# A six-layer cross-attention kernel: sums turned in 32x32 blocks, and two batches at a time from the fourth layer on

## What is computed

```python
q = (norm(x) @ Wq + bq); k = ctx @ Wk + bk; v = ctx @ Wv + bv      # 16 heads of 16
p = softmax(q @ k.T * 0.25)                                        # per head
x = x + (p @ v) @ Wo + bo                                          # CROSS and L3: norm before, none behind
x = x + relu(norm(x) @ f_w1 + f_b1) @ f_w2 + f_b2                  # FFN
```

## Time and profile before

| what | us |
|---|---|
| median of three runs | 1397.02 |
| the profiled execution | 1397.33 |
| its span in the trace | 1395.6 |
| TensorE busy | 1329.5 |
| VectorE busy | 994.2 |
| ScalarE busy | 898.1 |
| GpSimd busy | 603.0 |

### The profile page before, as it was taken

How to read it: one execution, slowest core, us unless ns; L and a number is a source line. 1 busy time by engine, 2 the same in 40 slices (tenths; PEclk the granted TensorE clock), 3 DMA queues, 4 the chain that set the end, 5 groups by cost and what they waited for, 6 DMA issues and landing times.

```text
span 1395.6 us, 46148 instructions
## 1 busy us (share of the span) xinstructions
PE 1329.5 (95%) x20076; PEld 1138.8 (82%) x20076; DVE 994.2 (71%) x1842; ACT 898.1 (64%) x1519; POOL 603.0 (43%) x767
## 2 busy tenths in 40 slices
PE   5999999999999999999999999999999999899997
PEld 4777888777887878888788878888999999778885
DVE  4778777888788777767776788886664446767774
ACT  4777777777777756666566776776434435667764
POOL 4944544576644643443334342222686665111100
PEclk9999999999999999999999999999999999999999
DMA  7211100010100000000000110000000000001000
GB/s 283 76 31 35 31 13 10 24 31 25 38 9 9 10 25 3 3 2 2 3 2 25 33 31 16 9 9 24 9 9 1 2 1 15 10 32 39 17 25 32
DMA packets 16609, 35.11 MB, mean 25 GB/s; under 512 B 2071, under 2 KB 7447, under 8 KB 15895
## 3 DMA queue, kind: packets, MB, share of 16 engines
q1 hardware_dynamic: 16407, 32.16, 7.1%
HBM read 27.96 MB, written 4.19 MB: 23 GB/s over the span
## 4 chain that ended last, share of the span: by engine, by line
PE 67%; DVE 14%; ACT 8%; POOL 5%; issue 3%; DMA 2%; SPq 0%; DVEq 0%; POOLq 0%; ACTq 0%
DVE s_nm L1101 9%; PE ps L717 8%; PE ps L782 8%; PE ps L744 6%; PE ps L796 6%; PE ps L810 6%; PE ps L606 5%; PE ps L659 5%; PE ps L761 5%; PE ps L631 4%; ACT s_PU L952 4%; PE ps L618 4%; PE ps L595 2%; PE ps L722 2%; DVE s_KH L1058 2%
## 5 line engine op out<-in xcount | busy, mean ns | idle before, releaser
L1101 DVE TENSOR_REDUCE s_nm<-ps 128x8 fp32r<-128x960 f32 (+1 forms) x352 | 395.8, 1168 | 88.4 <-PE ps L659 51.0
L952 ACT ACTIVATE s_PU<-ps 120x1024 f32<-120x1024 f32 (+1 forms) x288 | 280.6, 1024 | 105.5 <-PE ps L722 105.3
L717 PE MATMUL ps<-s_Qs,s_KH 32*120 32x256 f32 (+2 forms) x4608 | 184.8, 288 | 6.4 <-ACT s_PU L952 2.6
L1225 POOL TENSOR_TENSOR s_xs<-s_xs,s_rowv 128x512 f32<-128x512 f32 x96 | 123.9, 1291 | 151.8 <-ACT s_nt L857 133.6
L717 PEld LDWEIGHTS ps<-s_Qs,s_KH 32*120 32x120 f32 (+1 forms) x4608 | 151.5, 181 | 28.4 <-issue 5.1
L1254 POOL TENSOR_SCALAR s_rs<-s_mv 128x2 f32<-128x2 f32 x96 | 23.2, 242 | 325.4 <-DVE s_mv L1138 319.8
L961 ACT ACTIVATE s_Os<-ps 128x512 f32<-128x512 f32 x160 | 95.0, 598 | 102.8 <-PE ps L744 64.2
L782 PE MATMUL ps<-s_W,s_oT 128*128 128x256 f32 x960 | 135.3, 291 | 5.2 <-DVE s_oT L1030 3.5
L606 PE MATMUL ps<-s_xT,s_W 128*128 128x256 f32 x960 | 135.9, 292 | 3.1 <-POOL s_xT L1231 2.8
L744 PE MATMUL ps<-s_PU,s_Vp 120*32 120x256 f32 x2048 | 129.5, 384 | 9.2 <-ACT s_PU L952 7.2
L782 PEld LDWEIGHTS ps<-s_W,s_oT 128*128 128x128 f32 x960 | 120.0, 190 | 16.8 <-DVE s_oT L1030 7.0
(11 more groups left out here) (96 smaller groups left out, 2554.4 us busy)
## 6 DMA issues: line engine op xcount, KB each, us to landing
s_cf<-ctx_t SPq DMA_DIRECT2D x32, 240.0 KB, 2.6
s_ws<-weights SPq DMA_DIRECT2D x28, 256.0 KB, 2.7
s_nt<-x_t SPq DMA_DIRECT2D x16, 256.0 KB, 2.6
s_xs<-x_nat SPq DMA_DIRECT2D x4, 1024.0 KB, 11.3
out<-s_xs SPq DMA_DIRECT2D x16, 256.0 KB, 2.0
s_rowv<-rows SPq DMA_DIRECT2D x6, 512.0 KB, 3.9
s_mi<-mask SPq DMA_DIRECT2D x8, 120.0 KB, 3.4
s_who<-who SPq DMA_DIRECT2D x1, 128.0 KB, 3.2
```

Source lines behind the costliest of these rows:

```text
L717: e.matmul(banks[j][0:n, wide * x:wide * x + wide], kz[row[j], lk, g, c, k0:k0 + n], q[row[j], lq, g, qs_], start=(x == 0 and y_ == 0), st ...
L952: t = e.activation(P_of(i, k)[0:n, :, :], pair("B", i, k)[0:n, :, :], ACT.Exp, scale=0.25)
L1101: e.tensor_reduce(o, v, AX.X, ALU.max, negate=True).then_inc(sem["max"])
L1225: e.tensor_tensor(xs[:, b, :, :], xs[:, b, :, :], row2(layer, 0), ALU.add).then_inc(sem["pool"])
```

## The change

In CROSS and L3 (`TURNED`) `PVe`, `ON`, `ONe` and `OT` are gone. VectorE transposes each half of the sums in blocks of 32x32 straight out of PSUM (`X`), so that each block of 32 feature rows of a head lies beside its tokens; `rec` takes all reciprocals of the batch, GpSimd multiplies (`nmul`, 128x512), and `turn` transposes blocks of two heads' 16 sums back into `On`, in an order of features that the host's `mixed` gives to the output weights too. `OTh` and `OTl` read `On` in place of PSUM.

In CROSS, FFN and L3 (`TWOS`) `T`, `Th`, `Tl`, `Q`, `Qh`, `Ql` and the whole of `F1`, `Fa`, `Fv`, `Hl`, `F2` are made for two batches: matmuls of `Q` and `F1` run over 512 columns. `F1` goes in four quarters of 256 hidden features, and `F2` adds up over them for both batches.

`W` becomes ten single matrices, each reused by the matrix ten later, whose `Wh` waits for the last reader of the one it replaces. `Q` has four places in place of three, `Os` two whole batches in place of three halves, `K0` and `oT` one in place of two. All values of `WANT` (one for each kind of stage and layer) and several of `LONG` are new, `STAY` goes from 0.236 to 2.309, and some stages are tied to an order (`N` across layers, `Q`, `K`, `V`, `A` after the first `A`, L3's `K` behind the last `F1`). The wants and waits of SyncE's loads are those of before, but for an `xT` tile, which waits for the pair's `Xl` in a layer where pairs are made.

```diff
+TWOS = ("CROSS", "FFN", "L3")
+TURNED = ("CROSS", "L3")
...
-WSLOT = {n: k % 3 for k, n in enumerate(SETS)}
+
+MATRICES = [(n, m) for n in SETS for m in range(4)]
+PLACE = {x: k % 10 for k, x in enumerate(MATRICES)}
...
-STAY = 0.236
+STAY = 2.309
...
-        self.ring = {"Q": Slots(3), "KH": Slots(2), "K0": Slots(2), "PU": Slots(7), "Vp": Slots(2), "cT": Slots(2),
-                     "xT": Slots(2), "nt": Slots(2), "ws": Slots(2), "cf": Slots(1), "Os": Slots(3), "On": Slots(1), "oT": Slots(2), "nm": Slots(2), "mT": Slots(2),
+        self.ring = {"Q": Slots(4), "KH": Slots(2), "K0": Slots(1), "PU": Slots(7), "Vp": Slots(2), "cT": Slots(2),
+                     "xT": Slots(2), "nt": Slots(2), "ws": Slots(2), "cf": Slots(1), "Os": Slots(2), "Rc": Slots(2), "On": Slots(1), "oT": Slots(1), "nm": Slots(2), "mT": Slots(2),
...
+            for u in range(4 if i == pair else 0):
+                add("PE", "F1", u, after=[x_t, ("Wl", "F1", u)],
+                    rings=[("S", ("F1", i, u), [("Fv", i, 2 * u + 1)]), ("PU", ("F", i, u), [("Hl", i, u)]),
                            ("KH", ("H", i, u), [("F2", i, u)])])
                 for k in (2 * u, 2 * u + 1):
-                    add("ACT", "Fa", k, after=[("F1", i, u)] + [("wa", "F1", m) for m in range(4)])
+                    add("ACT", "Fa", k, after=[("F1", i, u), ("wa", "F1", u)])
                     add("DVE", "Fv", k, after=[("Fa", i, k)])
                 add("POOL", "Hl", u, after=[("Fv", i, 2 * u), ("Fv", i, 2 * u + 1)])
...
+                behind = [("F1", 5 * B - 2, 3)] if layer == "L3" else []
+                add("PE", "K", after=[ctx, (rest_of(layer), layer, 1)] + behind, long=1.43 if self_ else None,
...
+            turned = layer in TURNED
             for hf in range(2):
-                add("PE", "PV", hf, after=[("cap" if self_ else "exp", i, k) for k in half_pairs(i, hf)] + [("Ve", first, 0)],
-                    rings=[("MI", ("PV", i, hf), [("PVe", i, hf)]), ("Os", (i, hf), [("ON", i, hf)])], long=1.36 if self_ else None)
-                add("ACT", "PVe", hf, after=[("PV", i, hf)])
-                add("PE", "ON", hf, after=[("PVe", i, hf)],
-                    rings=[("MI", ("ON", i, hf), [("ONe", i, hf)])] + ([] if hf else [("On", i, [("OT", i, 0)])]))
-                add("DVE", "ONe", hf, after=[("ON", i, hf)])
-            p.stages["ON", i, 1].after.append(("ON", i, 0))
-            add("PE", "OT", after=[("ONe", i, 0), ("ONe", i, 1)], rings=[("MI", ("OT", i, 0), [("OTl", i, 0)]), ("oT", i, [("O", i, 0)])])
-            add("ACT", "OTh", after=[("OT", i, 0)])
+                add("PE", "PV", hf, after=[("cap" if self_ else "exp", i, k) for k in half_pairs(i, hf)] + [("Ve", first, 0)]
+                    + ([("PV", i, 0)] if hf else []), long=1.36 if self_ else None,
+                    rings=[("MI", ("PV", i, hf), [("X" if turned else "PVe", i, hf)])]
+                    + ([] if hf else [("Os", i, [("turn", i, 0)] if turned else [("ON", i, 0), ("ON", i, 1)])]))
+                if turned:
+                    add("DVE", "X", hf, after=[("PV", i, hf)])
+                else:
+                    add("ACT", "PVe", hf, after=[("PV", i, hf)])
+                    add("PE", "ON", hf, after=[("PVe", i, hf)] + ([("ON", i, 0)] if hf else []),
+                        rings=[("MI", ("ON", i, hf), [("ONe", i, hf)])] + ([] if hf else [("On", i, [("OT", i, 0)])]))
+                    add("DVE", "ONe", hf, after=[("ON", i, hf)])
+            if turned:
+                add("DVE", "rec", after=[("X", i, 0), ("X", i, 1)], rings=[("Rc", i, [("nmul", i, 0)])])
+                add("POOL", "nmul", after=[("rec", i, 0)])
+                add("DVE", "turn", after=[("nmul", i, 0)], rings=[("On", i, [("OTl", i, 0)]), ("oT", i, [("O", i, 0)])])
+            else:
+                add("PE", "OT", after=[("ONe", i, 0), ("ONe", i, 1)], rings=[("MI", ("OT", i, 0), [("OTl", i, 0)]), ("oT", i, [("O", i, 0)])])
+            add("ACT", "OTh", after=[("turn" if turned else "OT", i, 0)])
...
-        W = [sb(f"W{i}", [128, 2, 4, 2, 256], f32r) for i in range(3)]
+        W = [sb(f"W{i}", [128, 2, 2, 256], f32r) for i in range(10)]
+        K0 = [sb(f"K0{i}", [128, 2, 256]) for i in range(1)]
-        Os = [sb(f"Os{i}", [128, 2, S]) for i in range(3)]
+        Os = [sb(f"Os{i}", [128, 4, 8, 32]) for i in range(2)]
+        oT = [sb(f"oT{i}", [128, 2, 2, S], f32r) for i in range(1)]
...
-                            t = e.matmul(m[:, g * 256:g * 256 + 256], wv(layer, cw, 0)[:, k, 128 * g:128 * g + 128], xT_of(i)[:, cx, k, :],
+                            t = e.matmul(v[:, g, :], wv(layer, cw, 0)[:, k, 128 * g:128 * g + 128], xT_of(i)[:, cx, k, :],
...
+                w.wait_ge(*w_ready("F1", u))
+                for h in range(2):
                     for c, (cw, cx) in enumerate(PARTS):
                         for k in range(2):
-                            t = e.matmul(o, wv("F1", cw, mt // 2)[:, k, 128 * (mt % 2):128 * (mt % 2) + 128], x[:, cx, k, :],
+                            t = e.matmul(v[:, h, :], wv("F1", cw, u)[:, k, 128 * h:128 * h + 128], xT_of(i)[:, cx, k, :],
...
+            def F2(i, u):
+                hs = H_of(i, u)
+                w.wait_ge(sem["pool"], pool_ops["Hl", i, u])
+                w.wait_ge(*w_ready("F2", u))
+                for x in (i, i + 1):
+                    if not u:
+                        empty("F2", x)
+                    for q in range(2):
+                        for k in range(2):
+                            for c, (ch, cw) in enumerate(PARTS):
+                                at = 256 * (x - i) + 128 * q
+                                t = e.matmul(bankM("F2", x)[:, 256 * q:256 * q + 256], hs[:, ch, k, at:at + 128], wv("F2", cw, u)[:, k, :],
+                                             start=(u == 0 and k == 0 and c == 0 and q == 0), stop=(u == 3 and k == 1 and c == 2 and q == 1))
...
+                if layer_of(i) in TURNED:
+                    w.wait_ge(sem["turn"], nth("turn", i))
+                    src = On[slot("On", i)][:, :, :].rearrange("p a n -> p (a n)")
+                else:
+                    w.wait_ge(sem["OT"], nth("OT", i))
+                    src = bankM("OT", i)
...
+                was = had_place(n, m)
+                if was is not None:
+                    last = readers(*was)
+                    w.wait_ge(sem[last[0][0]], max(nth(*x) for x in last))
...
+            def X(i, hf):
+                for x in sums_free(i):
+                    w.wait_ge(*x)
+                w.wait_ge(sem["PV"], nth("PV", i, hf))
+                e.transpose(Os_of(i, hf).rearrange("p g n -> p (g n)"), bankM("PV", i, hf)).then_inc(sem["X"])
+            def rec(i):
+                was = ring["Rc"].before[i]
+                w.wait_ge(sem["X"], max(nth("X", i, hf) for hf in range(2)))
+                if was is not None:
+                    w.wait_ge(sem["pool"], pool_ops["nmul", was, 0])
+                o = Os[slot("Os", i)][:, :, :, :].rearrange("p g m c -> p (g m) c")
+                e.reciprocal(Rc[slot("Rc", i)][:, :].rearrange("p (h o) -> p h o", o=1), o[:, :, 16:17]).then_inc(sem["rec"])
+            def turn(i):
+                for x in On_free(i):
+                    w.wait_ge(*x)
+                w.wait_ge(sem["pool"], pool_ops["nmul", i, 0])
+                o = Os[slot("Os", i)]
+                for hf in range(2):
+                    t = e.transpose(On[slot("On", i)][:, hf, :], o[:, 2 * hf:2 * hf + 2, :, 0:16].rearrange("p g m c -> p m g c"))
+                t.then_inc(sem["turn"])
...
+            def nmul(i):
+                o = Os[slot("Os", i)][:, :, :, :].rearrange("p g m c -> p (g m) c")
+                w.wait_ge(sem["rec"], nth("rec", i))
+                behind()
+                rc = Rc[slot("Rc", i)][:, :].rearrange("p (h o) -> p h o", o=1)
+                e.tensor_tensor(o[:, :, 0:16], o[:, :, 0:16], rc.to_broadcast([128, 32, 16]), ALU.mult).then_inc(sem["pool"])
...
+    def mixed(w):
+        return w.reshape(2, 2, 4, 16, D).transpose(0, 2, 1, 3, 4).reshape(D, D)
```

## The result

The changed kernel takes 1362.43 us (median; 1360.68 to 1365.09) where the kernel before, run beside it, takes 1397.36: ratio 0.9754, 95% interval 0.9736 to 0.9772. The forecast was 1347, range 1318 to 1388. The profiled execution has a span of 1360.7 us, 34.9 less than before.

What follows compares the result with a forecast made beforehand. TensorE was taken to set the time in all layers, VectorE next. 1395.6 - 17.6 (CROSS) - 20.8 (L3) - 6 (FFN) + 2 (end) - 8 (order) = 1345.2 us of span; forecast 1347, range 1318 to 1388.

Steps and rivals of the forecast that it cites:

- rival B: Block transposes on VectorE run at the upper bound (`X` 1.149 us), so VectorE bounds CROSS and L3: 1363 us; chance 0.13.
- VectorE's share in CROSS: Sign that the forecast is right: VectorE busy above 93% in CROSS, against 80% before.
- Step 1: In CROSS and L3 TensorE loses two `ON` and the `OT`: 1.30 us a batch, 41.6 us over 32 batches.
- Step 2: VectorE in CROSS and L3 takes 2.60 us a batch for the turning, net +1.02 after what it loses and pairing.
- Steps 3 and 4: Matmuls over 512 columns for two batches: `Q` gives 0.09 us a batch, `F1` in FFN 6 us (0 to 8).
- Step 5, CROSS: CROSS falls from 12.90 to 11.8 us a batch, 0.3 charged for VectorE's nearness: 17.6 us gained (11 to 22).
- Step 5, L3: L3 gains 1.3 us a batch, 20.8 us (14 to 22); at the very end 2 us are lost.
- Step 6: New `WANT` and larger `STAY`: two fewer switches of array cut a batch, -8 us in layers one to three.
- Rival A: Everything is cashed: CROSS and L3 follow TensorE, FFN gains 8, three switches a batch go: 1328 us; chance 0.13.
- rival C: New order worse in layers one to three (+16 us), or single buffers bite: 1371 to 1394 us; chance 0.15.
- Step 7: Fewer buffers for `oT`, `K0`, `Os` and `W`, and longer load queues, are covered by early planning: nothing charged.
- Rival D: VectorE stalls at `turn` for GpSimd's `nmul`, 4 us a batch, so TensorE waits too: 1419 us; chance 0.12.

Runs made afterwards that it cites:

- experiment 2: Changed kernel, same order: VectorE reads each bank of sums once more, 1389.91 us; `OTl` cut to 16 columns, 1363.03 us; `Tl` cut to 16 columns, 1362.66 us.
- experiment 1: Changed kernel, planned anew, with neither CROSS nor L3 turned by VectorE, 1413.04 us; with only L3 turned, 1395.52 us.

## Why the prediction was right, and what was off by 15 us

The forecast's range holds the result, its own narrower range (1335 to 1358) does not, and the measured 1362 is almost rival B's 1363, by another way: the number alone would have picked the wrong mechanism. Of the signs it named, VectorE's share in CROSS came to 90% and not above 93%, and layers one to three grew longer.

**The bound** held: TensorE, with VectorE next.

**Step 1, turning leaves TensorE.** Right. In CROSS the steps of `ON` and `OT`, less the waits behind them, were 21.9 us in all, in L3 23.7; forecast 20.8 a layer.

**Step 2, VectorE's price.** Right by the nearest rows: a batch pays 2 x 0.705 + 0.335 + 2 x 0.418 = 2.58, forecast 2.60. `OTl` out of `On` has a mean of 0.768 instead of 0.686, but its median is 0.686 still: five of the 32 took 0.92 to 1.72 us. All five overlap an instruction of GpSimd, as three of the other 27 do; whether GpSimd is the cause was not tried. Over one pair VectorE rose from 20.84 to 21.80, 0.48 a batch, less than the +1.02 of the sum, in part because neighbours overlap in the records: the two transposes of a `turn` that begins at 1347.37 are busy for 0.76 us together, not 0.84. **Rival B** falls with it: no `X` near 1.149 us was seen. The Trainium skill, "VectorE: DVE Perf Modes", section "The three transpose paths", has 311 ns for 128x128 in bf16; here 512 columns of fp32 out of PSUM took 0.705, so 0.18 for 128 of them, and the measurement decides.

**Steps 3 and 4, 512 columns.** Right in kind, a third in size: against the run with halves 12 matmuls of 512 columns save 0.06 to 0.07 us, so some 5 ns a matmul where 15 was taken. `Q` of a pair steps 853.74 - 850.75 = 2.99, where two of the earlier trace rows step 1.60 each, and most blocks of `F1` step 2.79 to 2.87 instead of 2.93: more than the width gives, so the rest came with the order and with one block in place of two. FFN gained 4.6, forecast 6, and 1.7 of it is the width; that the sum came near is partly luck.

**Step 5, CROSS: the first term that was mis-sized.** 11.9 us gained, forecast 17.6 (11 to 22). I had TensorE's content at 11.51 a batch and charged 0.3 for VectorE's nearness. The content is 23.65 / 2 = 11.82, and VectorE is not what adds to it (experiment 2). In the pair shown, against the one of the kernel before, `PV` steps 4.07 instead of 3.74 as its halves stand apart, `M` 0.68 instead of 0.44 as it now ends at a cut, `K` 1.54 instead of 1.45, and the four `A` 3.86 instead of 3.30; the two in a row have 2.12 of it, where two step 0.78 and 0.87 elsewhere, and the run with the short `Tl` shows in the same block what the stall inside is, a bank that ScalarE still reads. Together 1.2 a pair, against the 2.6 that turning gave; `O`, `T` and `Q` give some 0.3 back. The step treated the rest of the list as unchanged. That the removed blocks left gaps which others filled at a worse place is not shown: with `ON` and `OT` back (experiment 1) the rest of CROSS takes as long, with its losses elsewhere (`A` 36.0 us in all where the changed kernel has 32.2, `PV` 32.4 where it has 36.9). They are losses of the new order with its pairs and buffers. The 0.3 a batch for VectorE's nearness had no row behind it: TensorE's idle time grew by 0.23 a pair, so 0.12 a batch, and the runs with less VectorE work gained nothing.

**Step 5, L3.** Right, in part by luck: 20.1 us in the ledger with the end included, forecast 20.8 - 2. Between the first and the thirteenth `y` of L3 lie 13.0 us a batch before (1209.48 to 1365.88) and 11.9 after (1198.53 to 1341.80), forecast 11.8; that is 1.1 a batch where 1.3 was forecast, 17.5 us in sixteen, and the rest lies at the layer's two ends. The end, forecast as 2 us lost, gained instead. From the last `PV` to the last `y` it took 1392.47 - 1383.13 = 9.3 us and takes 1357.59 - 1349.98 = 7.6 from its last half: the first half's `X` is done before that, and the last `O` steps 1.71 instead of 2.97. The table of stretches says why, first before, then changed:

```profile
1388.00:1393.00 5.00, 2.96 (x13) 2.64 (x12) 1.22 (x2) 0.60 (x1) 0.00 (x0) 0.66 0.00 0
```

```profile
1355.00:1359.00 4.00, 1.67 (x12) 1.49 (x12) 1.39 (x2) 0.01 (x1) 0.00 (x0) 1.00 0.04 15
```

In the kernel before that last block ran partly at the lower level of the clock (0.66 granted); now it runs at the upper. Counted from the end of the last `exp` (1383.86 and 1349.84) the gain at the end is 8.61 - 7.75 = 0.86 us, less than the 1.26 by which the last `O` is shorter: without the clock the new links would have lost some 0.4.

**Step 6, the order: the second mis-sized term, and the larger.** Forecast -8 in layers one to three from fewer cuts; measured +2.1 (+5.6 in L0 and L1, -3.5 in SELF). A higher `STAY` was to mean fewer cuts; there are 409 of them in these layers instead of 375. At 0.09 each (`A` before another scores block steps 867.53 - 866.75 = 0.78, before another cut 871.10 - 870.23 = 0.87) 34 more make 3.1. But the layers do not follow their cuts: L0 and L1 have 9 more and lost 5.6, SELF has 25 more and gained 3.5. So the count of cuts was the wrong measure of an order, and what else the new one changed there stays open; a part of L0 is the clock, granted at 0.83 over the changed kernel's first 40 us against 0.96 before. The mistake was to read one number of a planner apart from the wants found with it: with `STAY` at 0.236 there would be 685, so it does lower cuts within this set of wants, but between the two sets it says nothing. **Rival A** falls with this, and of **rival C** the direction held in L0 and L1, far from its 16 us.

**Step 7, single buffers.** Right as far as waits show: ScalarE's `OTh` stood for `turn` and never for `O`, `K0` for TensorE alone. What the order pays because it is planned around them, no run shows. **Rival D** (a stall at `turn`) had its place and not its size: 7.3 us over both layers, 0.2 a batch where 2.6 was its deciding point; `nmul` takes 1.08.

By terms, measured less forecast: layers one to three +10.1, CROSS +5.7, FFN +1.4, L3 with the end -1.3: 15.9 of the 15.4 between 1362.4 and 1347; the rest is weights and rounding.

## What to carry to other kernels

Price a moved operation by the nearest row of equal size and source; that held within 3% for the block transposes here (the small reciprocal took 12% less, `nmul` 16% less than priced). Where the order of the work is made by a planner, hold its order for a part of the kernel that has a price of its own: the same instructions cost 27 us more in the kernel before and 28 in the changed one under an order that nobody had searched, and 9 to 18 under searched ones, where the change brought 35. So a variant that has to be planned anew measures its order first and its idea second, and the planner's own time is the first look; it does not rank searched orders, as the three searches show. And when blocks are taken off the bound engine and the rest is ordered anew, count what the remaining blocks lose in the new order (here 1.2 against 2.6 us a pair), not only the blocks themselves.

## What the runs showed of the hardware that was not expected

A stall of TensorE cost more than itself here. In the run with the added reading, TensorE stood for VectorE for 1.44, 0.78, 0.75, 1.58 and 0.69 us between 1185 and 1201 us. Its granted clock was 0.83 and 0.75 over the two stretches from 1188 to 1196 us, 1.00 from 1196 to 1200, and 0.61 and 0.54 over the next two. The timeline and the last of these stretches:

```profile
1198.92 0.97 PE L819 MATMUL ps<-s_Qs,s_KH 32*120 32x256 f32 x24 [1.58 <-DVE s_Os L1216]
1203.02 2.92 PE L720 MATMUL ps<-s_cT,s_W 128*128 128x240 f32 x12
1205.86 1.64 PE L761 MATMUL ps<-s_KH,s_Qs 32*128 32x240 f32 x24
```

```profile
1204.00:1208.00 4.00, 4.00 (x44) 3.33 (x45) 0.44 (x1) 3.10 (x7) 0.00 (x0) 0.54 0.00 0
```

At 0.54, near the 1.2 GHz level, `K` steps 1205.86 - 1203.02 = 2.84 instead of 1.54, `A` 1.57 instead of 0.87. Over L3 of that run, from 1190 to 1390 us, the stretches below full clock add up to 12.6 us of clock not granted, against 1.7 in the changed kernel: an estimate, worked out from ten-microsecond stretches (length times what was missing to 1.00), that puts about half of L3's 20.2 us on the clock. The clock also makes foreign orders dearer than their idle time: 28 us for `STAY` 0.236, with 12.6 of added idle and, by the same estimate, 14.2 us of clock not granted behind the first 40 us, against 1.7.
